# Last layer of a four-layer graph network: the third head is masked by VectorE behind its exponential, and the denominators come ahead of the heads' products

## The reference, cut to what matters

```python
Q = einsum('bnd,hde->bhne', x, Wq); K = ...Wk; V = ...Wv
scores = einsum('bhne,bhme->bhnm', Q, K) / sqrt(32)
scores = where(adj > 0, scores, -inf)
attn = softmax(scores, axis=-1)
heads = einsum('bhnm,bhme->bhne', attn, V)
x = layernorm(x + concat(heads) @ Wo.T + bo)
```

## Time and profile before

| | |
|---|---|
| time before, median of 3 runs | 747.95 us (746.05 to 750.06) |
| the profiled execution's own time | 748.71 us |
| its span in the trace | 744.6 us |
| mean granted TensorE clock | 0.979 |
| busy: PE, DVE, ACT, POOL | 92%, 83%, 75%, 53% |
| last layer, steps 0 to 31 | from 483.80 us to the end |

### The profile page before, as it was taken

How to read it: one execution, slowest core, us unless ns; L and a number is a source line. 1 busy time by engine, 2 the same in 40 slices (tenths; PEclk the granted TensorE clock), 3 DMA queues, 4 the chain that set the end, 5 groups by cost and what they waited for, 6 DMA issues and landing times.

```text
span 744.6 us, 25853 instructions
## 1 busy us (share of the span) xinstructions
PE 686.7 (92%) x8484; PEld 507.2 (68%) x8484; DVE 620.2 (83%) x1782; ACT 559.8 (75%) x1266; POOL 394.8 (53%) x591
## 2 busy tenths in 40 slices
PE   5999999999988889999779999899999999999892
PEld 4677777777765667677568999766676666676561
DVE  2589999999898699999988888877778787878865
ACT  3576777777756899999678999777777778787572
POOL 4478778877886344444351112355464645555431
PEclk9799999999999999999999999999999999999997
DMA  7234434443320122232114332312222222222201
GB/s 219 84 120 125 113 105 122 119 120 101 113 69 15 28 36 36 35 35 35 15 46 121 88 88 72 65 16 44 59 47 49 56 49 56 47 58 44 50 35 53
DMA packets 34908, 51.97 MB, mean 70 GB/s; under 512 B 4388, under 2 KB 14376, under 8 KB 34856
## 3 DMA queue, kind: packets, MB, share of 16 engines
q1 hardware_dynamic: 20600, 34.36, 14.9%
q0 software_dynamic: 13968, 16.82, 13.9%
q10 hardware_dynamic: 288, 0.13, 0.1%
HBM read 51.32 MB, written 8.39 MB: 80 GB/s over the span
## 4 chain that ended last, share of the span: by engine, by line
PE 71%; DVE 18%; issue 5%; ACT 3%; DVEq 1%; POOL 1%; DMA 1%; SPq 0%; ACTq 0%; POOLq 0%
PE banks L751 9%; PE banks L1310 6%; PE banks L738 5%; PE banks L707 5%; PE banks L759 5%; PE banks L1651 4%; PE banks L1677 4%; PE banks L1662 4%; DVE pp L979 4%; PE banks L1625 4%; PE banks L1635 4%; PE banks L1630 3%; PE banks L1669 3%; PE banks L728 3%; PE banks L1318 3%
## 5 line engine op out<-in xcount | busy, mean ns | idle before, releaser
L626 DVE SCALAR_TENSOR_TENSOR pp<-banks,floor,adj 128x1024 f32<-128x1024 f32 x128 | 159.5, 1266 | 6.4 <-PE banks L738 5.4
L1405 POOL TENSOR_TENSOR pp<-pp,adj 128x512 f32<-128x512 f32 x64 | 73.4, 1162 | 129.1 <-ACT pp L1448 129.1
L1448 ACT ACTIVATE pp<-banks,nobound 128x512 f32<-128x512 f32 x128 | 81.5, 696 | 3.6 <-PE banks L1651 1.9
L751 PE MATMUL banks<-pp,yv 128*17 128x128 f32 x2048 | 82.8, 280 | 0.7 <-issue 0.5
L864 POOL TENSOR_TENSOR yres<-oo,x 128x512 f32 (+1 forms) x32 | 40.5, 1264 | 73.9 <-DVE oo L997 73.9
L533 ACT COPY rows<-banks 128x640 bf16<-128x640 bf16 x64 | 44.3, 692 | 42.5 <-PE banks L728 42.5
L1310 PE MATMUL banks<-w2b,xt 128*128 128x256 f32 x256 | 60.6, 380 | 3.0 <-ACT xt L1182 3.0
L751 PEld LDWEIGHTS banks<-pp,yv 128*17 128x17 f32 x2048 | 45.6, 98 | 15.6 <-issue 2.0
L738 PE MATMUL banks<-rows 32*128 32x128 bf16 x1024 | 51.5, 221 | 5.1 <-DVE pp L626 5.0
L897 ACT ACTIVATE x<-yres,nmr,rstd 128x128 f32 (+1 forms) x128 | 55.7, 490 | 0.0
L452 POOL TENSOR_TENSOR oo<-turned,rall 128x512 f32<-128x512 f32 x32 | 33.8, 1057 | 37.1 <-DVE rall L632 37.1
(11 more groups left out here) (214 smaller groups left out, 1921.6 us busy)
## 6 DMA issues: line engine op xcount, KB each, us to landing
xt<-in_xt SPq DMA_DIRECT2D x32, 256.0 KB, 2.8
adj<-in_adjt SPq DMA_DIRECT2D x32, 256.0 KB, 2.7
x<-in_x SPq DMA_DIRECT2D x32, 256.0 KB, 2.7
adj<-in_adjt POOLq DMA_DIRECT2D x64, 128.0 KB, 3.0
adj<-in_adj POOLq DMA_DIRECT2D x32, 256.0 KB, 3.0
out_ngd<-yres SPq DMA_DIRECT2D x32, 256.0 KB, 2.0
ident<-in_ident ACTq DMA_DIRECT2D x1, 64.0 KB, 2.2
w0t<-in_w0t SPq DMA_DIRECT2D x1, 64.0 KB, 2.0
```

Of the source, the lines that this page charges most:

```text
L626: nc.vector.scalar_tensor_tensor(pp[:, g], S[g % 2][:, :].rearrange("p (h n) -> p h n", n=N), floor[:, slot:slot + 1], adj[:, slot, g:g + ...
L751: ins = nc.tensor.matmul(O[32 * h:32 * h + w, c:c + N], yv[:, slot % 2, g * H + 4 * half + h, :], pp[:, g, 4 * half + h, :], start=True, s ...
L1405: nc.gpsimd.tensor_tensor(pp[:, slot % 2, h], pp[:, slot % 2, h], adj[:, slot], ALU.mult).then_inc(s["pm"], 1)
L1448: nc.scalar.activation(pp[:, slot % 2, h], S[h][:, :], ACT.Exp, bias=k["nobound"][:, :], scale=SCALE).then_inc(s["p"], 1)
```

## The change

In the last layer VectorE gets a new operation, `mask(t)`: it multiplies head 2's exponentials by the adjacency, both in SBUF, behind `evac_k(t+1)` and ahead of `finish(t-1)`; it waits for the third exponential of the step and signals the new semaphore `vm`. TensorE's `far` x `nota` product is left for head 3 alone. `denominators(t)` now stands ahead of `attend(t)`, and the waits for exponentials and masks move with it. The load of the adjacency waits for `vm` too, because VectorE now reads `adj` there.

```diff
         def load_adj(n, slot):
             need(pool, s["nota"], n - 3)
             need(pool, s["pm"], 2 * (n - 3))
+            need(pool, s["vm"], n - 3)
...
+        def mask(n, slot):
+            need(dve, s["p"], H * n + 3)
+            nc.vector.tensor_tensor(pp[:, slot % 2, 2], pp[:, slot % 2, 2], adj[:, slot], ALU.mult).then_inc(s["vm"], 1)
...
             if in1:
                 evac_k(t + 1, a1)
+            mask(t, slot)
             if inc:
                 finish(t - 1, c0)
...
         def scores(n, slot):
             need(pe, s["nota"], n + 1)
-            need(pe, s["p"], H * (n - 1) + 2)
-            for h in range(2, H):
-                need(pe, s["p"], H * (n - 1) + h + 1)
-                nc.tensor.matmul(S[h][:, :], far[:, :], nota[:, slot % 2, :], start=True, stop=False, skip_group_check=True)
+            need(pe, s["p"], H * n)
+            nc.tensor.matmul(S[3][:, :], far[:, :], nota[:, slot % 2, :], start=True, stop=False, skip_group_check=True)
...
-                    ins = nc.tensor.matmul(S[h][:, c], kt[r, slot % 2, c], qt[r, slot % 2, c], start=(h < 2), stop=(h < 2 or g == NG - 1),
+                    ins = nc.tensor.matmul(S[h][:, c], kt[r, slot % 2, c], qt[r, slot % 2, c], start=(h < 3), stop=(h < 3 or g == NG - 1),
...
         def attend(n, slot):
-            need(pe, s["p"], H * (n + 1))
-            need(pe, s["pm"], 2 * (n + 1))
             need(pe, s["va"], n + 1)
...
         def denominators(n, slot):
+            need(pe, s["p"], H * (n + 1))
+            need(pe, s["pm"], 2 * (n + 1))
+            need(pe, s["vm"], n + 1)
...
+            denominators(t, slot)
             attend(t, slot)
-            denominators(t, slot)
```

More of the change, by code:

```diff
@@ L1380, in heads @@
     on = sb("on3", [D, 2, NG * N], F32)
-    s = {n: sem(f"l3_{n}") for n in ("set ln xt_tr xt q qt kk kt v va rise pm nota xb link sq half var lvar root out s p o den log rec on "
+    s = {n: sem(f"l3_{n}") for n in ("vm set ln xt_tr xt q qt kk kt v va rise pm nota xb link sq half var lvar root out s p o den log rec on "
                                      "w y_out").split()}
```

## The result

The changed kernel takes 753.75 us (median of 7 runs, 750.3 to 755.42) against 747.95 for the kernel before: 1.0064 times as long, 95% interval 1.0041 to 1.0086. Run again beside other kernels it stood at 1.0048 [1.0025, 1.0071]. The two intervals overlap around +0.5%; 751.4 was forecast, which is +0.46%. The sign and the size are right, and what had to be found out is whether the reasons are.

What follows compares the result with a forecast made beforehand. TensorE was taken to bound the kernel at 7.60 us a step, with VectorE 0.30 in hand. Loop +2.9, one collision +1.2, outside the loop -1.0 and +0.3 gave +3.4 us: median 751.4, range 743 to 757.

Steps and rivals of the forecast that it cites:

- One `far` product less: TensorE, each step: one product fewer saves 0.21 us, making the TensorE-only period 7.39 instead of 7.60.
- The order of denominators and `attend`: TensorE: the same instructions in another order, priced at nothing, bounds -0.05 and +0.05 us.
- The mask's length: VectorE's new product: taken as 0.69 us, of which 0.61 occupies VectorE; bounds 0.5 to 0.75.
- Held by GpSimd: VectorE's mask waits for GpSimd's masks until 4.65 and ends 0.56 later; `finish` at 5.13, not 4.21.
- the first rival: VectorE's mask is not held by GpSimd and starts at 3.94: period 7.44, 743.4 us; chance 0.14.
- The mask gets in ahead of `xb`: When GpSimd's masks end at 4.65, VectorE's waiting mask goes before GpSimd's next instruction, `xb`.
- the third rival: `xb` gets the port ahead of VectorE's mask, `finish` starts at 6.34: period 8.33, 765 us; chance 0.08.
- What is late next: Work behind `finish` delays `divide` to 2.27 and the projection to 3.12: period 7.73, +2.9 us over 24 steps.
- `invert` held to 3.5: VectorE's `invert` falls inside GpSimd's first mask and waits to 3.5; keys' copy and mask still reach their place.
- The second collision: With `divide` at 2.6 or later, GpSimd's first mask holds the last piece of `result`: one step in 24, +1.2 us.
- Outside the loop: Steps 0, 1, 26 to 31: five gain the full 0.21 us, -1.0; step 28's flag work costs +0.3.
- The sum: Whole kernel: +3.4 us, giving 752.1 in the profiled execution and 751.4 as a median.

Runs made afterwards that it cites:

- kernel with the old order: The changed kernel with `attend` ahead of the denominators again, waits moved with it: 753.76 us, 1.0077 of the kernel before, period 7.86.
- `xb` first: Against the kernel with the SBUF mask behind `finish`, GpSimd runs `xb` ahead of its two masks: 740.2 us, period 7.43.
- the product done twice: Against the kernel with the mask from PSUM ahead of `finish`, that product is also done into a spare tile: 758.26 us, period 7.94.

## Why the prediction was right, point by point

**One `far` product less: right.** 0.21 forecast, 0.22 measured (7.60 to 7.38 without the mask).

**The order of denominators and `attend`: right.** Priced at nothing; alone 0.9985 [0.9964, 1.0006] and the same period to 0.01.

**The mask's length: right.** 0.69 forecast from `divide`, 0.69 measured with GpSimd's masks out of the way, 0.67 from PSUM.

**Held by GpSimd: right, and shown from three sides.** The mask was to end 0.56 behind GpSimd's second and ended 0.55 behind it. It is not held when its first input is in PSUM (period 7.55), when GpSimd has no masks (7.47), or when GpSimd issues a DMA at that moment (7.43). By the Trainium skill, "SBUF — State Buffer", section Who interferes with whom, two SBUF inputs contend with a reading GpSimd instruction and the first to issue keeps the port; the traces agree: 1.04 us beside GpSimd, 0.69 without it, 0.67 with one input in PSUM. The Trainium skill, "Advanced Engine Details and Errata", section VectorE Performance Modes, does not list this case; a reader of it alone would have taken the first rival, 743.4.

**The mask gets in ahead of `xb`: right.** `xb` stretched to 1.73 us says that it waited instead. The other order was measured only in the kernel with the mask behind `finish`. Its 765.4 us beside the third rival's 765 is a coincidence: the rival's price came through a late `finish`, the measured one through the denominators' wait for `vm` alone. What `xb` ahead of the mask would cost in the changed kernel's own order was not measured.

**What is late next, P = 7.73: right.** 7.74 measured, `divide` at 2.49 and 2.08 in turn where the working had their mean, 2.27. The halving holds: 0.60 more of VectorE makes 0.29. Not foreseen was a second way back of the same length: in the late steps the transposes, too, wait for `normalize` (0.29 idle at 621.43). It took nothing here, since the projection then comes at 622.95 and `divide` allows it at 622.14 + 0.85 = 622.99; but whoever shortens only `result` and `divide` will find it.

**`invert` held to 3.5: the hold was right, and its consequence was dropped.** In the two steps shown it ended at 3.74 (622.74 + 0.65 - 619.65) and 3.64 (630.33 + 0.96 - 627.65). I wrote that the mask still reaches its place in time, which is true of the changed kernel, and then priced the first rival as if the mask could start at 3.94. It issues at 4.17. With only the mask free of GpSimd, the rival was mis-sized: 7.55 in place of 7.44, with 746.57 in place of 743.4. Its sign held only just: 0.9975 [0.9953, 0.9996]. The hold of `invert` also shows that two inputs in SBUF are not what it takes: `invert` and the pieces of `result` read one tile in SBUF and write to SBUF, and both are held (up to 1.27 and 1.35 us, against 0.28 and 0.34). The instructions with an input in PSUM (`divide`, the keys' copy, `finish`) stay at 0.67 to 0.69 us in the loop, beside GpSimd's products too.

**The second collision: mechanism right, what pushes a step into it wrong.** It was put at a `divide` of 2.6 or later, and the 0.08 by which some steps have their first exponential later was to push it over. The timeline of step 26 of the changed kernel:

```profile
681.58 0.10 PEld L1648 LDWEIGHTS banks<-nota,far 128*128 128x128 bf16 x1 [0.20 <-issue]
...
683.03 2.12 DVE L1567 TENSOR_SCALAR yres<-yres,both,inv  x4
683.92 2.27 POOL L1406 TENSOR_TENSOR pp<-pp,adj 128x512 f32<-128x512 f32 x2 [3.00 <-ACT pp L1449]
...
685.07 0.68 DVE L1533 TENSOR_TENSOR on<-banks,rec 128x512 f32<-128x512 f32 x1
...
690.51 0.10 PEld L1648 LDWEIGHTS banks<-nota,far 128*128 128x128 bf16 x1 [0.20 <-issue]
```

`divide` at 3.49, as worked out, and a step of 8.93. The last piece of `result` started at 683.81 (the last and longest of the 96 pieces below), 0.11 ahead of GpSimd's recorded start, and was held all the same. All pieces, duration lowest/median/highest in ns:

```profile
L1567 DVE TENSOR_SCALAR yres<-yres,both,inv x96: 333/341/1346, 504.9 to 683.8; - x96
```

In the late step shown at the start, the last piece stood in the same place, 2.23 after the `far` load, but GpSimd's mask at 2.42 (622.07 - 619.65), and the piece ran free. In step 26 the mask was at 2.34. So it is an early first exponential that makes the collision, and a late one that spares the step. The late one comes in the first step of each round of the loop (steps 2, 6, 10 and so on: 1.64 of the step, against 1.56 in the others), which is also where `divide` is latest. Step 26 would be the next of these, but it is written out, its first exponential is at 1.56, and the collision comes. With GpSimd at 2.34 it sets in at a `divide` of 2.49; with GpSimd at 2.42, at 2.57. The kernel with the old order shows the second edge: both last pieces at 2.31 were held, those at 2.28 and 2.29 not.

One such step was counted in 24 and one came, in the profiled execution and in its repetition, in step 26, the first one behind the loop. Its 1.2 us stand in the sum, but not in the loop. That it is one was partly luck: the prediction held none or three as possible and didn't have the reason that picks this step.

**Outside the loop: the sum right to 0.1 us, its parts less so.** +0.3 - 1.0, and the collision's 1.2, make +0.5. Measured: 58.0 us of the layer outside these 24 periods before (240.5 - 182.5), 58.6 after (244.3 - 185.7), +0.6. The step with the collision is 1.3 longer (8.94 against 7.60), step 28 is 0.04 shorter (13.04 against 13.08) where 0.3 more was forecast, and the other steps give back 0.7 where 1.0 was. Steps 27 and 29 have the full gain of one product (7.38 against 7.60). The three errors nearly cancel, which is luck.

**The sum.** +3.4 was forecast, the last layer shows +3.8: 3.2 in the loop for 2.9, 0.6 for 0.5. The medians of the two comparisons, 1.0064 and 1.0048, are +4.8 and +3.6 us of 747.95. The term that was too small is the loop's, 0.133 a step for 0.12; that is below what the medians can tell.

## What to carry to other kernels

Work put into the idle time of an engine is not free because the engine waits there: ask what it reads, and what the neighbour on the same port is running in that microsecond. A product of VectorE with both inputs in SBUF belongs beside a GpSimd that is idle or issuing DMAs, or one of its inputs belongs in PSUM; here the places of these instructions alone lay between 765 and 740 us with the same work. An instruction that is held can also push the next one into its own collision, as `invert` did. In a chain that closes over two steps, an insertion costs half of its length in the period, and the other half moves `divide` towards the next collision.

## What was not expected of the hardware

**The edge of the hold is not the recorded start, and not the same for all.** An `invert` recorded 0.03 us ahead of GpSimd's mask runs free at 0.28 us, and GpSimd's two masks take 2.38 together (the rows at 604.44 and 604.47); one that comes 0.11 behind is held to the end, 1.20 us (545.65 against 545.54). Between them the recorded starts don't settle it: with the mask behind `finish` one 0.06 behind runs free, and in the kernel with the old order three recorded 0.03 behind are held for 1.27 us. A piece of `result` 0.11 or 0.12 us ahead is held, one 0.13 ahead is not. Why the edge of the one lies ahead of the recorded start and that of the other does not was not tried.

**TensorE's clock behind the same idle time differs from kernel to kernel.** In step 28 TensorE waits for `on` behind the flag work. The kernel before:

```profile
703.14 1.95 PE L1677 MATMUL banks<-w3ot,on 128*128 128x128 f32 x8 [3.55 <-DVE on L1528]
704.88 1.91 PE L1625 MATMUL banks<-xt,w3q 128*128 128x512 f32 x2
```

The kernel with the mask from PSUM behind `finish`:

```profile
697.24 1.16 PE L1684 MATMUL banks<-w3ot,on 128*128 128x128 f32 x8 [3.56 <-DVE on L1533]
698.24 1.02 PE L1632 MATMUL banks<-xt,w3q 128*128 128x512 f32 x2
```

The same idle time (3.55 and 3.56 us) and the same products, at 1.95 and 1.91 us against 1.16 and 1.02: the 1.2 GHz level against the 2.4 GHz one. The granted clock was 0.55 of full speed from 703 to 706 us in the first kernel, and 1.00 over the whole step in the second. The step took 13.08 us before, 13.04 in the changed kernel, 11.21 in this one and 14.01 with the mask from PSUM ahead of `finish`; the ends of the range are 10.47 (`xb` first) and 14.28 (the product done twice). What decides it stays open. It is a reason to read the periods of the loop and not the spans: between two of these kernels up to 3.8 us can be this step's. It can be one reason why the four kernels between 740.2 and 741.3 us don't stand in the order of their periods (7.38 to 7.47).
